# Three B row buffers, 64-column tap weights, both residual adds as identity matmuls copied out by ScalarE, and new slots on every queue

## The reference

```python
x = x + mamba(layernorm(x))
x = x + ffn(layernorm(x))

# mamba: 4 heads of 128 channels, 16 states
x, z = split(h @ in_proj_w.T);  x = silu(conv4(x) + conv_b)
dt_r, Bm, Cm = split(einsum('hod,blhd->blho', xw, xh))
delta = softplus(einsum(dtw, dt_r) + dt_b);  A = -exp(A_log)
s = s * exp(d_t * A) + (d_t * u_t) * B_t          # over 1024 steps
y_t = sum_n(s * C_t)
out = ((y + x * Dskip) * silu(z)) @ out_proj_w.T

# ffn: every linear quantises input and weight in blocks of 16
h = silu(fp4_linear(v, w_gate)) * fp4_linear(v, w_up)
out = fp4_linear(h, w_down)
```

## Time and profile before

| | us |
|---|---|
| median of 3 runs (lowest, highest) | 4243.98 (4243.51, 4249.21) |
| profiled execution, own time | 4253.05 |
| its span, first to last instruction | 4251.1 |
| start of the first scan, start of the last | 84.91, 4152.17 |

### The profile page before, as it was taken

One profiled execution on the slowest core, in us unless ns is written; L12 is line 12 of the kernel. 1 busy time (PEld: TensorE's weight loads), 2 busy tenths in 40 slices (PEclk: granted clock), 3 DMA queues, 4 the chain that ended last, 5 costly groups with the idle time before them and its releaser, 6 DMA issues. The chain is left out here.

```text
span 4251.1 us, 67554 instructions
## 1 busy us (share of the span) xinstructions
PE 3945.4 (93%) x19884; PEld 1859.3 (44%) x19884; DVE 4060.8 (96%) x5684; ACT 3639.7 (86%) x6807; POOL 3941.9 (93%) x2461
## 2 busy tenths in 40 slices
PE   4789999999999999999999999999999999999997
PEld 1234444444444444444444444444444444444445
DVE  6899999999999999999999999999999999999994
ACT  5888888888888888888888888888888888888874
POOL 5999999999999999999999999999999999999993
PEclk8999999999999999999999999999999999999999
DMA  3555555555555555555555555555555555555550
GB/s 107 200 192 192 186 187 191 186 189 188 185 187 190 188 185 191 184 189 191 188 184 191 184 187 190 185 185 190 192 183 190 188 186 190 189 186 187 183 184 23
DMA packets 307411, 772.79 MB, mean 182 GB/s; under 512 B 37734, under 2 KB 89062, under 8 KB 307046
## 3 DMA queue, kind: packets, MB, share of 16 engines
q1 hardware_dynamic: 305344, 766.31, 54.0%
q10 hardware_dynamic: 1702, 2.16, 0.2%
HBM read 743.16 MB, written 25.17 MB: 181 GB/s over the span
## 5 line engine op out<-in xcount | busy, mean ns | idle before, releaser
L752 POOL TENSOR_TENSOR prod<-state,cs 128x1024 f32<-128x1024 f32 x1024 | 2411.5, 2367 | 10.6 <-issue 10.3
L743 POOL TENSOR_TENSOR brow<-brow,du 128x512 f32<-128x512 f32 x640 | 817.2, 1277 | 189.6 <-DMA brow<-b_rows 179.2
L486 ACT ACTIVATE decay<-delta,aneg 128x512 f32<-128x512 f32 x1408 | 962.4, 716 | 22.5 <-DVE state L1008 20.7
L987 DVE TENSOR_TENSOR db<-db,du 128x512 f32<-128x512 f32 x1408 | 962.3, 683 | 17.8 <-PE db L1056 16.9
L1071 PE MATMUL ybank<-prod,ident 64*64 64x512 f32 x3584 | 899.3, 610 | 9.9 <-DVE hh L905 6.4
L1071 PE MATMUL cross<-prod,ident 64*64 64x512 f32 x3584 | 899.2, 610 | 0.0
L1008 DVE TENSOR_TENSOR_SCAN state<-decay,carry,db 128x512 f32<-128x512 f32 x704 | 883.1, 1263 | 0.0
L1008 DVE TENSOR_TENSOR_SCAN state<-decay,db 128x512 f32<-128x512 f32 x704 | 841.6, 1204 | 6.3 <-PE bank_b L1344 6.3
L1056 PE MATMUL db<-pieces,sel 128*128 128x512 bf16 x1408 | 541.3, 385 | 48.9 <-DVE state L1008 42.9
L486 ACT ACTIVATE db<-delta,aneg 128x512 f32<-128x512 f32 x640 | 437.8, 684 | 47.6 <-DVE state L1008 44.5
L1160 PE MATMUL bank_a<-wd,ht 128*128 128x256 f32 x1536 | 406.6, 390 | 57.7 <-ACT hh L503 56.0
(11 more groups left out here) (144 smaller groups left out, 7643.7 us busy)
## 6 DMA issues: line engine op xcount, KB each, us to landing
cs<-c_rows SPq DMA_DIRECT2D x1024, 512.0 KB, 3.7
brow<-b_rows SPq DMA_DIRECT2D x640, 256.0 KB, 3.9
xin<-in_hidden SPq DMA_DIRECT2D x128, 128.0 KB, 3.8
xres<-in_hidden SPq DMA_DIRECT2D x128, 128.0 KB, 3.8
out_x<-ot SPq DMA_DIRECT2D x128, 128.0 KB, 3.9
c_rows<-xdbl SPq DMA_DIRECT2D x128, 32.0 KB, 3.4
b_rows<-xdbl SPq DMA_DIRECT2D x128, 32.0 KB, 3.2
win<-in_win_t SPq DMA_DIRECT2D x1, 1024.0 KB, 5.1
```

Of the source, the lines that this page charges most:

```text
L486: act.activation(out, delta[:, w.mod(2), :], ACT.Exp, scale=aneg[:, w.mod(HEADS), n:n + 1]).then_inc(done, 1)
L743: pool.tensor_tensor(brow[:, s, :], brow[:, s, :], du[:, w.mod(2), :], ALU.mult).then_inc(db_pool, 1)
L752: pool.tensor_tensor(prod[:, r, :, :], state[:, 2 * p:2 * p + 2, :], cs[:, c, :, :], ALU.mult).then_inc(weighted, 1)
L987: dve.tensor_tensor(t[:, :], t[:, :], du[:, gu % 2, :], ALU.mult).then_inc(db_done, 1)
```

## The change

1. `WEIGHED_ROWS` goes from 2 to 3: three `brow` buffers, so a B row's DMA waits for the scan three POOL-states back. To make room, `cdiag` holds only 64 columns for each tap (`blocks_of_one` is a helper of two stacked 64x64 identities), and the last tap becomes two 64x64 matmuls on the two diagonal quadrants.
2. First residual: PE adds `ident` x `xres` (128x256) to the group in `bank_a`; ACT copies the bank to `x1` and takes the row sum in the same instruction. DVE's add (L945) and ACT's separate sum (L666) are gone.
3. Second residual: PE adds `ident` x `x1` after `down`; ACT copies `bank_a` to `ot`. DVE's add (L966) is gone.
4. The slots of almost all jobs on PE, ACT, POOL, DVE and the order on SP are new.

```diff
-WEIGHED_ROWS = 2
+WEIGHED_ROWS = 3
...
-        cdiag = sb("cdiag", [HEADS, TAPS, P])
+        blocks_of_one = sb("blocks_of_one", [Q])
+        cdiag = sb("cdiag", [HEADS, TAPS, Q])
...
             def conv_tap(v, k):
-                last = pe.matmul(pbank[:, :], cdiag[:, v.mod(HEADS), k, :], x[:, k:k + CH],
-                                 start=False, stop=(k == TAPS - 1), skip_group_check=True)
+                for r in range(2):
+                    rows = slice(r * Q, (r + 1) * Q)
+                    last = pe.matmul(pbank[rows, :], cdiag[rows, v.mod(HEADS), k, :], x[rows, k:k + CH],
+                                     start=False, stop=(k == TAPS - 1), tile_position=(r * Q, r * Q),
+                                     skip_group_check=True)
...
             def project(t, heads):
+                    pe.wait_ge(ld_res[t.mod(2)], t.div(2, 16, 16))
+                    pe.matmul(bank_a[:, 0:DM], ident[:, :], xres[:, t.mod(2), :], start=False,
+                              stop=True).then_inc(op_mm, 1)
...
             def down(t, ks):
+                    pe.matmul(bank_a[:, 0:DM], ident[:, :], x1[:, t.mod(4), :], start=False,
+                              stop=True).then_inc(dn_mm, 1)
...
                 # ScalarE
+                if t := due("post", 16):
+                    act.wait_ge(op_mm, t.val(plus=1))
+                    wait(act, centred2, t.val())
+                    wait(act, dn_mm, t.val(plus=-3))
+                    act.activation(x1[:, t.mod(4), :], bank_a[:, 0:DM], ACT.Copy, accum_out=sum2[:, :]).then_inc(x1_done, 1)
+                if t := due("post", 73):
+                    act.wait_ge(dn_mm, t.val(plus=1))
+                    act.wait_ge(ot_free[t.mod(2)], t.div(2, 16, 16))
+                    act.activation(ot[:, t.mod(2), :], bank_a[:, 0:DM], ACT.Copy).then_inc(o_done, 1)
...
                 # VectorE
-                if t := due("post", 15):
-                    dve.tensor_tensor(x1[:, t.mod(4), :], bank_a[:, 0:DM], xres[:, t.mod(2), :],
-                                      ALU.add).then_inc(x1_done, 1)
-                if t := due("post", 74):
-                    dve.tensor_tensor(ot[:, t.mod(2), :], bank_a[:, 0:DM], x1[:, t.mod(4), :],
-                                      ALU.add).then_inc(o_done, 1)
```

More of the change, by code:

```diff
@@ new lines, in step @@
+                if t := due("post", 53):
+                    act.wait_ge(h_round, t.val(4, 2))
+                    act.activation(cross[:, 0:HALF], hv[t.mod(2)][:, HALF:INNER], ACT.Abs, scale=POWER).then_inc(h_abs, 1)
+                if due("post", 37) and not due("pre", 21):
+                    act.preload_act_table_set("exp_and_others")
+                if t := due("post", 21):
+                    act.wait_ge(v_norm, t.val(plus=1))
+                    wait(act, h_op, t.val(2))
+                    act.activation(bank_b[:, 0:DM], v2, ACT.Abs, scale=POWER).then_inc(v_abs, 1)
@@ L1313, in side @@
                               start=True, stop=True).then_inc(xd_mm, 1)
[L1314 to L1317 removed]
+                if t := due("post", 71):
+                    down(t, (0, 1))
+                if t := due("post", 71):
+                    down(t, (2, 3))
+                if v := due("pre", 7):
+                    pe.wait_ge(xnt_done, v.div(4, 4, 4))
+                    wait(pe, delta_done, v.val())
+                    in_proj(v, 0, 0)
@@ new lines, in side @@
+                if t := due("post", 38):
+                    up(t, 1)
+                if w := due("scan", 20):
+                    sum_up(w, (7,))
+                if w := due("scan", 4):
+                    spread_b(w.val(NST, 5))
+                if v := due("pre", 20):
+                    pe.wait_ge(mid_done, v.val(plus=1))
+                    pe.matmul(pbank[:, :], less[:, 1, :], mid[:, :], start=False, stop=True,
+                              skip_group_check=True).then_inc(res_mm, 1)
@@ new lines, in side @@
+                if t := due("post", 29):
+                    pe.wait_ge(v_quant, t.val(plus=1))
+                    if peeled and t.val() == 0:
+                        pe.wait_ge(xnt_done, 11)
+                    else:
+                        wait(pe, h_op, t.val(2))
+                    for k in range(KM):
+                        last = pe.transpose(bank_b[:, k * P:(k + 1) * P], v2_eps[:, k * P:(k + 1) * P], ident[:, :])
+                    last.then_inc(v_tp, 1)
+                if w := due("scan", 13):
+                    spread_b(w.val(NST, 15))
```

610 lines of the change are left out of this document (280 added, 330 removed).

## The result

| | before | changed |
|---|---|---|
| median, us (lowest, highest; 4 runs each) | 4243.74 (4236.04, 4249.21) | 4094.73 (4093.89, 4097.52) |
| profiled execution, its span | 4253.05, 4251.1 | 4097.52, 4094.2 |
| mean granted TensorE clock | 0.989 | 0.995 |

The ratio is 0.9651, with a 95% interval of 0.9635 to 0.9668: faster by 149 us, where the forecast had 101.

A forecast was written before the change was run, and what follows sets the result against it. DVE bounds late units, POOL's loop through SP's queue and the B row early ones. 31.79 - 30.95 = 0.84 us over some 120 units saves 101: profiled 4152, median 4143 us, range 4105 to 4208.

The forecast's parts named there:

- the length of the units after: Per unit after the change: late 30.89 us (DVE), early 30.6 (PE; POOL 30.5), mean 30.75.
- the allowance: Per unit: 0.2 us added for waits that stay, taking the mean from 30.75 to 30.95.
- the baseline: Unit before: 31.79 us, first to last scan over 128 units, matched by one early and one late unit averaging 31.80.
- the ends at zero: Setup and end of the kernel: taken as zero change, 5 us either way.
- The wait for the B row: POOL's early-unit wait for state 4's B row, 1.67 us, came from its place behind C pairs in SP's queue.
- ACT's wait for `rstd`: ACT's scaling waited for POOL's `rstd`, 220.6 us, 1.9 a unit; the new ACT order would remove it.
- The narrow tap: Last tap on PE as two quadrant matmuls: 0.43 us for both together, so it costs nothing.
- B: Only deleted work returns; a new wait keeps the early unit: 4206, or 4167 if the early one gains; chance 0.2.
- C: PE is no bound and the waits vanish: 30.7 us a unit, 4113 us; chance 0.08.
- A: The forecast itself for the whole kernel: 4143 us, own range 4115 to 4175; chance 0.55.
- D: Slower: PE's waits for ACT stay because `bank_a` waits for ACT twice a tile; 4347, half-way 4290; chance 0.1.
- E: The narrow tap's quadrants run one after the other: 0.86 us more on PE, 31.45 a unit, 4203; chance 0.03.

The follow-up runs named there:

- a_pe_plus: The changed kernel with PE doing the first matmul of every `down` step twice, about 0.43 us more a unit: 4133.5 us, ratio to before 0.9709.
- a_pe_less: The changed kernel without the identity matmul of `x1` behind `down`, PE 0.43 us less a unit: 4067.9 us, ratio to before 0.9555.
- b_row4: The kernel before with one DMA moved on SP, the B row of state 4 ahead of the first two C pairs: 4145.8 us, ratio 0.9738.
- b_sp: The kernel before with all of SP's new order alone, still two B row buffers: 4136.1 us, ratio 0.9704.
- b_old_slots: The whole change on the kernel before, except the new slots on PE, ACT, POOL and DVE: 4097.6 us, ratio 0.9617.
- b_ident_row4: The kernel before with identity residuals copied out by ACT and state 4's B row moved ahead of the C pairs: 4110.7 us, ratio 0.9652.
- a_sp_old: The changed kernel with the old SP order, three buffers kept: 4895.2 us, ratio to before 1.1492.
- b_ident: The kernel before with both residuals as identity matmuls copied out by ACT, old slots and old SP order: 4251.6 us, ratio 0.9974.

## Why the prediction was right or wrong

**Right: the length of the units after.** Late units were to be 31.53 - 0.64 = 30.89 with DVE busy throughout; they are 30.89. Early ones were to be PE's, 30.6 with POOL at 30.5; they are 30.70 and PE's, as a_pe_plus and a_pe_less show. The mean was to be 30.75 before the allowance; it is 30.77. That it came so close is in part luck: 30.70 and 30.89 average to 30.80, and the one short length of each batch row, 30.45, takes off the rest. PE's work without the identities was put at 29.7; with full taps and both identities it is 30.49 or less, so 29.63.

**Wrong: the baseline.** The step that failed is "the mean of the two, 31.80, is the 31.79 above, so they stand for all". 31.79 was the time from the first scan to the last over 128. The first six lengths in it have less tile work (29.4 each), and the stretches ahead of them and at the end, 55.5 us, count as two units. The steady units took 31.97. That the single early unit of 32.07 and the single late one of 31.53 average to 31.80 was chance: another early one took 30.60, and the late ones were 31.9 on average. 0.18 in 120 units is 22 us. b_row4 shows the error in it: late units were stretched by the same B row. A small slip stands beside it: "30.4 + 1.67 = 32.07" takes the wait from one early unit and the rest from another, whose busy time is 30.48.

**Wrong: the allowance.** "For waits that stay I add 0.2" is 24 us. What stays on DVE is 14.1 + 5.5 + 4.5 us in 117 units, 0.2 indeed, but it lies in the early units, whose length PE sets. It was counted on top of a bound that already covers it.

**Wrong: the ends at zero.** The first six units gave 10 us, mostly by the SP order and the third buffer (table above: 176.0, 169.7, 164.6), the end 4. Against that, the profiled execution lay 3 above the median and not 9. In sum: 101 + 22 + 24 + 14 - 1 (setup) - 6 = 154, and with the units' 30.77 in place of 30.75 (2) it is 152, against 149 measured. No single term puts the time outside the range: 22, 24 and 13 us all went one way.

**The mechanism.** The wait for the B row was read rightly as a matter of its place in the queue. What the prediction did not see is how much of the change that one place is: 0.90 of the 1.20 us a unit (b_row4). The identities are 0.23, and only once the row is early; the rest of SP's order 0.09 with the identities in (nothing without them: b_row4 31.07, b_sp 31.08), and 7 us at the start; third buffer and narrow taps cost 0.09 in the unit and give 4 us at the start; the new slots give 0.07. The prediction gave the third buffer a share ("with three buffers row 4 waits for the scan of state 11, not 14, and it is asked for ahead of the C pairs"); only the second half of that sentence counts in the old slots. The mechanism was thus right where it said why the B row came late, and wrong in what it took the cure to need.

**ACT's wait for `rstd`.** The forecast credited the new ACT order. In b_sp and b_row4 ACT's order is the old one and the wait falls from 213.6 to 9.2 and 22.7, PE's for `delta` from 99.6 to 1.1 and 5.1. ACT was late since POOL was; the new order was not needed for it.

**The narrow tap** "costs nothing" is wrong by 0.21 us in an early unit, where PE is the bound. The reading of the pairs was right; weight loads of the changed kernel at the full clock, for the two halves of the last tap, each a pair of quadrants:

```profile
1868.11 0.14 PEld L1076 LDWEIGHTS pbank<-xlate,cdiag 64*64 64x64 f32 x2 [0.28 <-issue]
1868.54 0.14 PEld L1076 LDWEIGHTS pbank<-xlate,cdiag 64*64 64x64 f32 x2 [0.29 <-issue]
```

0.43 apart, as stated. So nearly all of the 0.21 lies not in the pair but at its two sides, between it and the 128x128 matmuls, as the two timelines above show. The prediction put these steps at nothing; its rows had only such pairs one behind the other. Why a step between the two shapes takes 0.10 longer no run shows.

**Rivals.** B (only the deleted work returns) fell: no new wait took the old one's place. C named PE as no bound; a_pe_plus, with 39 us more for 0.43 us of PE a unit, refutes that. The rule behind C, in the Trainium skill, "Perfetto Trace Analysis", section "Identifying the Most-Contended Engine", judges TensorE's headroom by MFU (the share of peak arithmetic) and by the busy share of its weight loads. Of MFU no view here has a figure. At 48% of the span the loads would leave it half free, and the trace disagrees: in an early unit 0.43 more work is 0.43 later. C's time, 4113, came nearer to the result than A's for a reason that is not its own. D (`bank_a` waits for ACT) is in the trace at 2.3 us in all, for the copy of `ot`; with the old slots PE waits 18 to 33 us there for the copy of `x1` (b_old_slots, b_ident_row4), still far from 1.2 a unit. E needed 0.86 for the narrow tap; it was a quarter of that, and for another reason: the quadrants ran together.

## What to carry to other kernels

A queue that issues in order is a resource with a critical path of its own: before adding buffers or deleting engine work, ask for each late transfer whether it waits for its buffer or for its neighbour in the queue, and try the one move. Work taken off a busy engine pays nothing while a loop elsewhere sets the pace, and pays in full afterwards, so such edits are measured on top of the fix and not beside it. Take the baseline of a steady unit from many end markers, leaving out the first ones, and test which engine bounds it by adding and removing a known piece, since busy shares of 96 and 97% did not tell PE, POOL and DVE apart.

## What the runs showed of the hardware

The kernel before has short stretches at a lower granted clock, and the changed kernel has none between 400 and 4000 us. A window of the kernel before, columns as in the earlier trace rows, with the clock in the third column from the end:

```profile
2150.00:2160.00 10.00, 9.00 (x42) 4.45 (x44) 8.22 (x15) 8.67 (x17) 10.00 (x7) 0.83 0.46 148
```

In six stretches of 10 us between 2000 and 4000 the clock was 0.83 or 0.84 on average. Read in steps of 1 us, the first of them has PE busy for 0.71, 0.38, 0.72 and 0.28 of four successive steps at the full clock, 2.4 GHz, then fully busy for some three at 0.50, 1.2 GHz, and then at the full clock again; the two others that were read so (from 2213 and 2469 on) look the same. So PE's waiting came first and the lower clock behind it. The units there took 33.16, 33.54 and 33.53, 1.3 to 2.1 us more than their neighbours. The changed kernel has PE at 96% of the span; a_sp_old, where PE waits most, has such a stretch in about every third 10 us. The clock does not explain the differences between the kernels: b_ident and b_row4 have no such stretch between 400 and 4000 either, and b_ident has before's unit of 31.96. Nor does it explain why the medians of before ranged from 4243.7 to 4262.3 between groups while those of the changed kernel agreed to 0.1: within one group, runs of before with the same mean clock of 0.988 took 4255.4, 4261.4 and 4267.8. That cause stays open.
